# K^T of a two-kernel graph attention layer by way of DRAM and VectorE instead of TensorE, with the PSUM banks and the order of all queues rearranged

## The reference, cut to what matters

```python
z_l, z_g, v = h @ W_lang.T, h @ W_grav.T, h @ W_V.T
zn  = z_l / max(norm(z_l), EPS)
A_l = max(zn @ zn.T, 0) * not_eye
A_g = exp(-max(sq + sq.T - 2 * z_g @ z_g.T, 0) / (2 * sigma**2)) * not_eye
K   = w_l * row_stochastic(A_l * mask) + (1 - w_l) * row_stochastic(A_g * mask)
out = layernorm(h + (K @ v) @ W_O.T)
```

## Time and profile before

| | us |
|---|---|
| median of 3 runs (lowest, highest) | 718.54 (718.18, 722.65) |
| the profiled execution's own time | 718.95 |
| its span, first to last instruction | 717.2 |

### The profile page before, as it was taken

The page is one execution under the profiler, slowest core; times in us unless marked ns, Lnnn a source line. Parts: engine busy times, 40 slices in busy tenths (PEclk is TensorE's granted clock), DMA queues, the critical chain, the costliest instruction groups (busy, mean ns, idle before and its releaser), DMA issues.

```text
span 717.2 us, 10995 instructions
## 1 busy us (share of the span) xinstructions
PE 695.4 (97%) x3146; PEld 574.5 (80%) x3146; DVE 499.9 (70%) x1350; ACT 373.6 (52%) x707; POOL 122.8 (17%) x282
## 2 busy tenths in 40 slices
PE   9899999999999999999999999999999999999973
PEld 7688888888888888888888888888888888888852
DVE  4553877768677777778777776867777777866762
ACT  4333445646546554655645554654655464555545
POOL 3301011120212111030211112021211103021112
PEclk9999999999999999999999999999999999999998
DMA  9220534535553544444543445445443454353222
GB/s 288 49 60 32 153 105 117 154 110 156 142 150 113 151 131 124 154 124 125 152 138 120 132 131 151 125 126 154 136 137 122 124 154 124 96 154 96 67 89 95
DMA packets 105013, 90.75 MB, mean 127 GB/s; under 512 B 11040, under 2 KB 79136, under 8 KB 104992
## 3 DMA queue, kind: packets, MB, share of 16 engines
q1 hardware_dynamic: 104432, 88.93, 42.5%
q0 software_dynamic: 288, 1.05, 0.5%
q10 hardware_dynamic: 272, 0.52, 0.2%
HBM read 57.93 MB, written 32.54 MB: 126 GB/s over the span
## 4 chain that ended last, share of the span: by engine, by line
PE 95%; DVE 2%; ACT 1%; issue 1%; DMA 0%; POOL 0%; ACTq 0%; POOLq 0%; DVEq 0%
PE bank L956 90%; PE bank L1071 2%; PE bank L978 2%; PE bank L999 1%; DMA out_y<-y 0%; DVE p_lo L687 0%; ACT y L597 0%; ACT m_hi L510 0%; DVE y L863 0%; DVE m_lo L703 0%; ACT junk_a L589 0%; DVE work L793 0%; DVE hT_raw L673 0%; DVE hT_lo L681 0%; ACT v_hi L543 0%
## 5 line engine op out<-in xcount | busy, mean ns | idle before, releaser
L956 PE MATMUL bank<-hT_lo,m_hi 128*128 128x512 f32 x512 | 168.0, 389 | 0.0
L543 ACT CAST p_hi<-bank 128x512 fp32r<-128x512 f32 x128 | 74.6, 583 | 128.1 <-PE bank L956 128.1
L746 DVE TENSOR_TENSOR p_lo<-bank,p_hi 128x512 fp32r<-128x512 f32 x128 | 87.7, 686 | 57.8 <-ACT p_hi L543 56.3
L956 PE MATMUL bank<-hT_hi,m_lo 128*128 128x512 f32 x320 | 124.5, 389 | 0.0
L956 PEld LDWEIGHTS bank<-hT_lo,m_hi 128*128 128x128 f32 x512 | 96.1, 188 | 19.9
L956 PE MATMUL bank<-p_hi,hT_hi 128*128 128x512 f32 x256 | 101.2, 395 | 0.0
L956 PE MATMUL bank<-wvo_hi,hT_hi 128*128 128x512 f32 x256 | 100.5, 393 | 0.0
L956 PE MATMUL bank<-wvo_hi,hT_lo 128*128 128x512 f32 x256 | 100.4, 392 | 0.0
L956 PE MATMUL bank<-wvo_lo,hT_hi 128*128 128x512 f32 x256 | 100.1, 391 | 0.0
L956 PE MATMUL bank<-p_lo,hT_hi 128*128 128x512 f32 x256 | 100.0, 390 | 0.0
L543 ACT CAST v_hi<-bank 128x512 fp32r<-128x512 f32 x64 | 37.5, 587 | 102.4 <-PE bank L956 102.4
(11 more groups left out here) (105 smaller groups left out, 1226.8 us busy)
## 6 DMA issues: line engine op xcount, KB each, us to landing
x_blk<-in_x SPq DMA_DIRECT2D x128, 128.0 KB, 3.1
x_nat<-in_x SPq DMA_DIRECT2D x32, 512.0 KB, 4.5
out_y<-y SPq DMA_DIRECT2D x32, 512.0 KB, 3.1
x_spill<-xs SPq DMA_DIRECT2D x30, 512.0 KB, 4.0
xq<-x_spill SPq DMA_DIRECT2D x120, 128.0 KB, 3.6
r_row<-r_spill SPq DMA_DIRECT2D x32, 128.0 KB, 4.2
work<-in_L_gnn_W_grav SPq DMA_DIRECT2D x2, 512.0 KB, 6.5
y<-in_L_gnn_W_O SPq DMA_DIRECT2D x2, 512.0 KB, 8.3
```

What stands on the lines that cost most here:

```text
L543: nc.scalar.copy(dst, src).then_inc(proj_hi, 1)
L746: nc.vector.tensor_tensor(dst, src, hi.bitcast(F32), ALU.subtract).then_inc(proj_ready, 1)
L956: last = pe.matmul(dst, lhsT, rhs, start=(n == 0), stop=(n == len(steps) - 1))
```

## The change

K^T of all pairs but the last goes the way of X^T: `spill_k` writes K to DRAM, `return_k` reads it back in four DMAs with runs of 64 floats (256 bytes), and `turn_k` turns the 32x32 blocks on VectorE into the tile GAUSS, from which ScalarE and VectorE take the two parts. `kt_turned` takes the place of `kt_done`, and `work` and `adj_off` are laid out by blocks of 32 columns, with both row tiles side by side, so that `gram` is one instruction rather than two.

The two banks of K^T become free: projections (and the 22 units of the head) rotate over four banks, `k_times_v` has two. The four tiles of X follow each other, both `k_times_v` of graph 0 stand behind the second value tile, those of graph 1 behind all value tiles. The orders on VectorE, ScalarE, SyncE and GpSimd are rewritten: `inverse_masked`, `turn_x` and the first `gram` of graph 0 now stand at the end of the pair in which X was made, `gauss` of it as well. `spill_x` is two DMAs, one for each row tile; `store_r` writes single floats to rows of a transposed layout. adj is loaded into `r_row`, cleared on its diagonal there and copied to `adj_off` by GpSimd. The tail's order is rewritten too: `kt_hi_part(q, 1)` and `turn_k(q, 1)` fall into it, and `squares(q, 1)` stands behind the last `kt_hi_part`.

```diff
@@ buffers and banks @@
-        kt_hi = sb("kt_hi", [P, 2, NT, N], F32R)
-        kt_lo = sb("kt_lo", [P, 2, NT, N], F32R)
-        x_spill = nc.dram_tensor("x_spill", [2, NT, P, WIDE], F32)
-        r_spill = nc.dram_tensor("r_spill", [2, P, NT], F32)
+        kt_hi = sb("kt_hi", [P, 2, NT, NT, P], F32R)
+        kt_lo = sb("kt_lo", [P, 2, NT, NT, P], F32R)
+        x_spill = nc.dram_tensor("x_spill", [2, P // BLK, NT, BLK, WIDE], F32)
+        k_spill = nc.dram_tensor("k_spill", [2, NT, P, N], F32)
+        r_spill = nc.dram_tensor("r_spill", [2, NT, P], F32)
...
-        proj_bank = bank[0:3]
-        kv_bank = bank[3]
+        proj_bank = bank[0:4]
         x_bank = bank[4:6]
-        kt_bank = bank[6:8]
+        kv_bank = bank[6:8]
...
-            return (kv_bank, x_bank[0], x_bank[1], proj_bank[0])[2 * b + t]
+            return kv_bank[t] if b == 0 else proj_bank[t]
 
         def pbank(k):
 
-            return proj_bank[(PREP + k) % 3]
+            return proj_bank[(PREP + k) % 4]
...
@@ SyncE @@
-                sp.dma_start(x_spill[b].rearrange("u p f -> p u f"),
-                             xs[:, b].rearrange("p (u f) -> p u f", u=NT)).then_inc(spilled[b], 16)
+                for u in range(NT):
+                    sp.dma_start(x_spill[b].rearrange("i u c f -> u i c f")[u],
+                                 xs[:, b, u * WIDE:(u + 1) * WIDE]).then_inc(spilled[b], 16)
...
+            def spill_k(q, b):
+                if not live(q):
+                    return
+                sp.wait_ge(k_ready, upto(q, 4, 2 * b + 2))
+                sp.dma_start(k_spill[b].rearrange("h p f -> p h f"),
+                             wk(b, KER).rearrange("p (h f) -> p h f", h=NT)).then_inc(k_spilled[b], 16)
+
+            def return_k(q, b):
+                if not live(q):
+                    return
+                sp.wait_ge(k_spilled[b], 16 * (q + 1))
+                run = NT * BLK
+                for j in range(P // BLK):
+                    cols = k_spill[b].rearrange("h (i c) f -> c (h i) f", c=BLK)[:, :, run * j:run * (j + 1)]
+                    sp.dma_start(wk(b, COS)[j * BLK:(j + 1) * BLK].rearrange("c (k f) -> c k f", f=run),
+                                 cols).then_inc(kq_loaded[b], 16)
+
             def store_r(p, b):
                 sp.wait_ge(pool_steps, upto(p, 6, 3 * b + 1))
-                sp.dma_start(r_spill[b], rnorm[:, b]).then_inc(r_stored[b], 16)
+                sp.dma_start(r_spill[b].rearrange("t p -> p t").unsqueeze(2), rnorm[:, b].unsqueeze(2),
+                             allow_slow_non_contiguous=True).then_inc(r_stored[b], 16)
 
...
@@ SyncE, the order within a pair @@
                 return_x(q, 1)
+                spread_r(q, 1)
+                load_blocks(p + 1, 1)
+                load_x(q, 0)
+                load_x(q, 1)
+                spill_k(q, 0)
                 load_blocks(p + 2, 0)
+                return_k(q, 0)
+                spill_k(q, 1)
                 store(q - 1, 0)
-                load_blocks(p + 1, 1)
-                spread_r(q, 1)
-                load_x(q, 0)
                 store(q - 1, 1)
-                load_x(q, 1)
+                store_r(p, 0)
                 spill_x(p, 0)
-                store_r(p, 0)
+                return_k(q, 1)
+                spread_r(p, 0)
                 return_x(p, 0)
-                spread_r(p, 0)
                 spill_x(p, 1)
                 store_r(p, 1)
...
@@ GpSimd, the order within a pair @@
-                layer_norm(q - 1, 1)
-                inverse_norms(p, 0)
-                floors(p, 0)
-                mean(q, 0)
-                inverse_norms(p, 1)
-                floors(p, 1)
-                mean(q, 1)
-                layer_norm(q, 0)
+                for b in range(2):
+                    mean(q - 1, b)
+                for b in range(2):
+                    layer_norm(q - 1, b)
+                for b in range(2):
+                    inverse_norms(p, b)
+                    floors(p, b)
...
@@ ScalarE, kt_hi_part @@
-                act.wait_ge(kt_done, upto(q, 2, b + 1))
                 if live(q - 1):
                     act.wait_ge(out_done, upto(q - 1, 4, 2 * b + 2))
-                nc.scalar.copy(kt_hi[:, b], kt_bank[b][:].rearrange("p (t n) -> p t n", t=NT)).then_inc(kt_hi_ready, 1)
+                if is_last(q):
+                    act.wait_ge(kt_done, b + 1)
+                    nc.scalar.copy(kt_hi[:, b].rearrange("p t h n -> p h t n"),
+                                   x_bank[b][:].rearrange("p (h t n) -> p h t n", h=NT, t=NT)).then_inc(kt_hi_ready, 1)
+                else:
+                    act.wait_ge(kt_turned, upto(q, 2, b + 1))
+                    nc.scalar.copy(in_kt(kt_hi, b), wk(b, GAUSS)).then_inc(kt_hi_ready, 1)
...
@@ ScalarE, the order within a pair @@
                 proj_hi_part(p, 1)
+                squares(q - 1, 0)
                 proj_hi_part(p, 2)
-                normalise(q - 1, 0)
                 proj_hi_part(p, 3)
-                gauss(q, 0)
+                proj_hi_part(p, 4)
+                gauss_scaled(q, 0)
                 squares(q - 1, 1)
-                proj_hi_part(p, 4)
                 proj_hi_part(p, 5)
-                gauss_scaled(q, 0)
                 proj_hi_part(p, 6)
                 proj_hi_part(p, 7)
                 gauss(q, 1)
-                normalise(q - 1, 1)
-                kt_hi_part(q, 0)
-                turn_hi(p + 1, 1 - parity, 0)
+                normalise(q - 1, 0)
+                gauss_scaled(q, 1)
                 save_x(p, 0, 0)
                 save_x(p, 0, 1)
-                gauss_scaled(q, 1)
+                normalise(q - 1, 1)
                 centre(p, 0)
+                kt_hi_part(q, 0)
                 save_x(p, 1, 0)
                 save_x(p, 1, 1)
+                if is_last(p):
+                    return
+                turn_hi(p + 1, 1 - parity, 1)
+                proj_hi_part(p, 8)
+                proj_hi_part(p, 9)
+                centre(p, 1)
                 kt_hi_part(q, 1)
-                proj_hi_part(p, 8)
-                centre(p, 1)
-                proj_hi_part(p, 9)
-                if is_last(p):
-                    return
-                squares(q, 0)
-                turn_hi(p + 1, 1 - parity, 1)
                 proj_hi_part(p, 10)
                 proj_hi_part(p, 11)
-
+                turn_hi(p + 2, parity, 0)
+                gauss(p, 0)
...
@@ ScalarE, behind the last pair @@
             pair(p, 1)
+            centre(p, 1)
             gauss(p, 0)
+            proj_hi_part(p, 8)
+            proj_hi_part(p, 9)
+            gauss_scaled(p, 0)
+            kt_hi_part(q, 1)
+            gauss(p, 1)
             squares(q, 0)
-            gauss_scaled(p, 0)
+            kt_hi_part(p, 0)
             proj_hi_part(p, 10)
-            gauss(p, 1)
-            kt_hi_part(p, 0)
             normalise(q, 0)
+            gauss_scaled(p, 1)
             proj_hi_part(p, 11)
-            gauss_scaled(p, 1)
+            kt_hi_part(p, 1)
             squares(q, 1)
-            kt_hi_part(p, 1)
             normalise(q, 1)
-            squares(p, 0)
-            normalise(p, 0)
-            squares(p, 1)
-            normalise(p, 1)
+            for b in range(2):
+                squares(p, b)
+                normalise(p, b)
...
@@ VectorE, gram @@
-                for t in range(NT):
-                    dst = wk_h(b, (COS, GAUSS)[g])[:, :, t].rearrange("p h (j a) -> p h j a", a=BLK)
-                    ins = nc.vector.tensor_tensor(dst, dst, x_of(b)[:, :, :, g, t], ALU.add)
-                ins.then_inc(gram_ready, 1)
-
-            def gram_of_bank(q, b, g):
+                dst = wk_k(b, (COS, GAUSS)[g])
+                own = x_of(b)[:, :, :, g].rearrange("p u j t a -> p (u j) (t a)")
+                nc.vector.tensor_tensor(dst, dst, own, ALU.add).then_inc(gram_ready, 1)
...
@@ VectorE, turn_k and the low part of K^T @@
+            def turn_k(q, b):
+                if not live(q):
+                    return
+                dve.wait_ge(kq_loaded[b], BLKS * (q + 1))
+                dve.wait_ge(k_ready, upto(q, 4, 2 * b + 2))
+                nc.vector.transpose(wk(b, GAUSS).rearrange("p (t k c) -> p k t c", t=NT, c=BLK),
+                                    wk(b, COS).rearrange("p (k t a) -> p k t a", t=NT, a=BLK)).then_inc(kt_turned, 1)
...
+                    nc.vector.tensor_tensor(in_kt(kt_lo, b), wk(b, GAUSS), in_kt(kt_hi, b).bitcast(F32),
+                                            ALU.subtract).then_inc(kt_ready, 1)
...
@@ VectorE, the order within a pair @@
                 proj_lo_part(p, 0)
-                turn_x(q, 0)
+                gram(q, 0, L)
                 proj_lo_part(p, 1)
-                gram(q, 0, G)
+                cosine_masked(q, 0)
+                gauss_masked(q, 0)
+                row_factors(q, 0)
                 proj_lo_part(p, 2)
-                inverse_masked(q, 0)
                 proj_lo_part(p, 3)
```

(108 more changed lines are left out.)

165 lines of the change are left out of this document (86 added, 79 removed).

## The result

The changed kernel took 856.8 us (median of 4, 851.75 to 857.38) against 718.65 before: ratio 1.189, 95% interval [1.183, 1.195], slower by 138 us. The prediction said 706, with a range of 702 to 714. It was wrong.

The account below looks back on a forecast made before the run. It took what TensorE issues as the bound. Turns of K -13.3, head -1.2, first seam +0.8, tail +1.2 gave -12.5 us against 718.95: 706.4, as median 706.0; range 702 to 714.

Parts of the forecast that it names:

- place (3): Pair's seam on VectorE: low part of value tile 10 done 41.9, bank wanted 42.6, spare 0.6 us; X back 36.9.
- place (2): K of graph 1: return lands at 32.1, turn_k due 33.2, K^T split 35.1, wanted 37.2; spare on VectorE 2.1 us.
- a doubled return: K's return of graph 1 taking twice as long, landing at 34.1: still covered by the spare, 0 for TensorE.
- Rival B: Late return of K of graph 1 stops TensorE; a 9 us landing costs 2.4 us a pair, 740 us; chance 0.12.
- the 0.95 us a pair: TensorE's two turns of K, removed in pairs 1 to 14: 14 x 0.95 = 13.3 us, if nothing becomes late.
- The ends: Terms outside the loop: head -1.2 us, pair 0's seam +0.8 once, tail +1.2.
- the head: Start of the kernel: with four banks, units wait less for low parts; -1.2 us (0 to -2.7).
- The first seam: End of pair 0, shorter without K V: X comes back later than wanted; +0.8 us (0 to 2), once.
- The last pair: The tail, 68.4 us from the last pair's start to the end before: +1.2 us (-2 to +3).
- the text's own limit for the pair: Sign of a wrong prediction: last pair taking more than 72 us from its first projection to the end.
- The mis-sized term of the tail: TensorE's lower clock level after standing still ahead of graph 0's last K V: up to 1.8 us, +0.5 taken.
- That the end hangs on `normalise(q, 1)`: Tail: the end is set by normalise(q, 1), until 56.6 against 55.9 before, its store and the waiting residual; +0.7 us.

Follow-up runs that it names:

- e2: The changed kernel with r stored in pairs in the DRAM layout of the kernel before (128 writes of 8 bytes): 734.2 us, ratio 1.020.
- e1: The changed kernel with X spilled by four DMAs over 32 partitions each instead of two: 805.9 us, ratio 1.120.
- e3: The changed kernel with both edits, X spilled by four DMAs over 32 partitions and r stored in pairs: 710.1 us, ratio 0.987.
- e13: As e3, but in the tail ScalarE does squares(q, 1) and normalise(q, 1) ahead of the last kt_hi_part(p, 1): 705.8 us, ratio 0.981.
- e6: As e1, but GpSimd issues r's 256 single-float writes on its own queue rather than SyncE: 814.4 us, ratio 1.132.

## Why the prediction was wrong

**The step that failed** is place (3), with the landing of X's spill and of `store_r`: "lands by 31.5" and "takes 4.8 us in the median, 8.4 at the most". Those rows are of one DMA over 128 partitions and of 128 writes of 8 bytes. The change gave both another form, and I kept their durations. They measured 13.3 and 13.5 us with both forms changed; with only one changed it was 8.2 to 8.9 for the spill (e2) and 8.1 for the store (e1). The delay reached TensorE at place (2): K's return of graph 1 was issued at 409.30, that is T + 27.9 (26.7 was forecast, the pair starting at 381.37), but VectorE turned it at T + 42.1, where the landing had been put at 32.1 and even a doubled return at 34.1. In the sum both new forms were a term of nothing, with no upper bound of its own; counted from e3 the spill's was worth 24 us, the single floats' 96, and the two together 147.

The reading of the earlier trace rows was also loose: those are views of a whole tile, in which writes and reads of the DRAM buffer are mixed. The store of r alone had 5.6 us, not 4.8, and the spill of X 4.0; this is too little to matter.

The prediction names `store_r`'s 4 bytes beside what the Trainium skill says of small runs ("DMA: Bandwidth & Descriptors", Specifications), but it gave a bound only to K's returns. These cost no wait in e3: 2.7 us to landing, against 3.1 for X's. That is no evidence against the rule, since each of K's DMAs has half the bytes of X's (64 against 128 KB) in as many packets. The dear one was a 1 KB store.

**Rival B had the place, not the cause.** It said that K of graph 1 would stop TensorE when its return is late, at 740 us for a landing of 9 us. That is the wait in the trace (8.3 us ahead of `turn_k`), but the return is not slow by itself: e3 has the same return in time. B's price also left out the clock, 1.9 us a pair, and the chance of 0.12 was low for a chain in which two DMAs had changed form besides K's.

**What held.** On the engines the order came out as laid down: in the changed kernel's own trace `turn_k` of graph 0 starts at 406.42 - 381.37 = 25.0 in its pair where 24.5 was forecast, its duration is 0.71 us (0.65), the joined `gram` 0.69 (0.68). With the two DMAs put right the period is 39.9 us, as predicted, and TensorE never waits in the loop; the 0.95 us a pair are won (e3).

**The ends**, read in e3: the head brought 1.8 us (forecast 1.2; the second pair starts at 74.95 instead of 76.75). The first seam cost 2.1 us (forecast 0.8, at most 2). The last pair takes 72.5 us instead of 68.4, +4.1 (forecast +1.2, at most +3, and the text's own limit for the pair was 72). Sum: -13.3 - 1.8 + 2.1 + 4.1 = -8.9, and the spans differ by 717.2 - 708.2 = 9.0. The mis-sized term of the tail is the clock, taken at 0.5 and worth 3.4: the two K V stretches of twelve matmuls took 4.4 us rather than 2.7 each (675.13 to 679.54 and 685.41 to 689.85), the lower level having come soon after waits of 2.0 and 2.5 us. So e3's 710.1 lies inside the stated range, but 4 us above the forecast. That the end hangs on `normalise(q, 1)` was right; moving it gave 4.3 us (e13).

## What to carry to other kernels

A DMA whose access pattern changes is a new DMA: take nothing from the old one's landing time, however small it is, and ask what in the same queue and on the same engines stands behind it. Never scatter single floats to neighbouring addresses in DRAM from different partitions; write pairs, or let them start 8 bytes or more apart. Look at the outer dimension of both sides of a DMA: 32 and 128 were good here, 4 was not, and 16 was not tried. When a large rearrangement comes out slower, factor it: two small edits turned 1.19 into 0.99.

## What the hardware showed that was not expected

- 256 four-byte writes, 4 bytes apart in DRAM, cost 118 us over 32 stores of 1 KB (828.0 against 710.1); 8 bytes apart about 2 (712.3). They delay other queues' transfers as well (e6).
- TensorE's clock can fall behind a short wait. In e3 a wait of 2.0 us is followed by four matmuls at the usual distance and eight 0.43 us apart:

```profile
675.13 0.50 PE L1026 MATMUL bank<-v_hi,kt_hi 128*128 128x512 f32 x1 [2.02 <-DVE kt_lo L916]
...
676.55 0.63 PE L1026 MATMUL bank<-v_hi,kt_lo 128*128 128x512 f32 x1
```

The granted clock of that stretch (windows of e3: us, then busy times, the clock, DMA share, GB/s):

```profile
676.00:678.00 2.00, 2.00 (x7) 1.57 (x6) 2.00 (x7) 1.50 (x4) 0.00 (x0) 0.55 0.00 0
```

Two waits of 1.4 us in the tail of the kernel before, and one of 1.5 in that of e3, did not bring it down: the matmuls behind them start 0.23 us apart.
